# Middle passes of a two-layer decoder kernel: another order of calls on TensorE, ScalarE and VectorE, with key blocks around the turning of z0

## What is computed

```python
# layer 0
q, k, v = x @ kernel[0], x @ kernel[1], x @ kernel[2]      # 16 heads of 64
x = norm(x + softmax(q k / (d d h)) v @ WO)                # attention
x = norm(x + cross_attention(x, ctx))                      # 16 heads of 16, 120 context rows
x = norm(x + bitlinear(silu(bitlinear(x)) * bitlinear(x))) # rows quantized to 8 bit, weights to -1, 0, 1
# layer 1
h = norm(x); a = decay(h) @ (h @ Wv); x = x + sigmoid(h @ Wo) * a   # gated, causal
x = norm(x + mlp(norm(x)))
q = x @ Wq + bq; k1, k2 = ctx @ Wk1, ctx @ Wk2; v1, v2 = k1 @ Wv1, k2 @ Wv2
z0 = norm(q + softmax([q k1, q k2] / 16, axis=queries) [v1, v2]) * g0 + beta0
z1 = norm(z0 + relu(z0 @ Wo + bo)) * g1 + beta1;  x = norm(x + z1)
# coupled network: three cycles over the features, gf from the mean over the tokens
gf = sigmoid(g3(gelu(g2(gelu(g1(mean(x)))))))
for _ in range(3):
    tf = sigmoid(w4(gelu(w3(gelu(w2(gelu(w1(out))))))))
    out = out + (0.1 + range * (0.7 gf + 0.3 tf - 0.5) * 2) * twist(out)
x = norm(x + out)
```

## Time and profile before

| | us |
|---|---|
| median of 3 runs | 1095.97 (1095.93 to 1096.03) |
| the profiled execution, its own time | 1095.17 |
| its span, first to last instruction | 1093.4 |
| TensorE busy | 1023.6 (94% of the span) |
| VectorE busy | 793.0 (73%) |
| ScalarE busy | 629.3 (58%) |
| GpSimd busy | 310.2 (28%) |

### The profile page before, as it was taken

How to read it: one execution, slowest core, us unless ns; L and a number is a source line. 1 busy time by engine, 2 the same in 40 slices (tenths; PEclk the granted TensorE clock), 3 DMA queues, 4 the chain that set the end, 5 groups by cost and what they waited for, 6 DMA issues and landing times.

```text
span 1093.4 us, 19696 instructions
## 1 busy us (share of the span) xinstructions
PE 1023.6 (94%) x7216; PEld 686.6 (63%) x7224; DVE 793.0 (73%) x1854; ACT 629.3 (58%) x1720; POOL 310.2 (28%) x666
## 2 busy tenths in 40 slices
PE   9999999999989999999889999999988998799896
PEld 5577557855667655775557755786566675577563
DVE  3684886668697488657789578665869849865877
ACT  2583655476587257359468455646747816634933
POOL 1264202341056301242107420223104640124210
PEclk9999999999999999999999999999999999999998
DMA  9350000000010000000000000000000000000000
GB/s 338 83 170 1 20 1 10 1 1 1 1 40 1 20 2 10 1 1 1 1 20 21 1 20 1 10 1 1 1 0 11 12 1 1 1 1 0 2 1 20
DMA packets 16431, 22.78 MB, mean 21 GB/s; under 512 B 2256, under 2 KB 14032, under 8 KB 16208
## 3 DMA queue, kind: packets, MB, share of 16 engines
q1 hardware_dynamic: 15472, 20.85, 5.9%
q10 hardware_dynamic: 864, 0.68, 0.2%
HBM read 19.42 MB, written 2.10 MB: 20 GB/s over the span
## 4 chain that ended last, share of the span: by engine, by line
PE 62%; DVE 17%; ACT 12%; issue 5%; POOL 2%; DMA 1%; ACTq 0%; POOLq 0%; DVEq 0%
PE PS L542 9%; PE PS L970 4%; ACT work L1533 4%; PE PS L730 4%; PE PS L939 3%; PE PS L679 3%; PE PS L578 3%; PE PS L716 3%; ACT work L1787 3%; PE PS L565 2%; DVE maxx L2148 2%; PE PS L696 2%; PE PS L984 2%; DVE work L2165 2%; PE PS L1023 2%
## 5 line engine op out<-in xcount | busy, mean ns | idle before, releaser
L2628 POOL TENSOR_TENSOR rstd<-var,minus_half 128x2 f32<-128x2 f32 x64 | 45.8, 715 | 509.6 <-DVE var L1955 509.6
L1787 ACT ACTIVATE work<-PS,nmax 120x256 f32<-120x256 f32 x256 | 117.9, 484 | 13.6 <-DVE nmax L2443 12.6
L2443 DVE TENSOR_REDUCE nmax<-PS 120x2 f32<-120x512 f32 x128 | 82.5, 686 | 33.6 <-PE PS L970 32.5
L1533 ACT ACTIVATE work<-PS,nmax 128x256 f32<-128x256 f32 x176 | 81.6, 489 | 16.2 <-DVE nmax L2016 16.2
L2016 DVE TENSOR_REDUCE nmax<-PS 128x2 f32<-128x512 f32 x128 | 82.4, 679 | 10.9 <-PE PS L679 10.1
L2642 POOL TENSOR_SCALAR work<-work,inv 128x256 f32<-128x256 f32 x176 | 81.1, 479 | 0.0
L2623 POOL TENSOR_TENSOR pool_pause<-minus_half 128x1 f32<-128x1 f32 x96 | 28.5, 297 | 178.2 <-DVE inv L2023 92.4
L679 PE MATMUL PS<-work 64*128 64x256 f32 x512 | 72.2, 396 | 6.1 <-ACT work L1533 5.8
L1488 ACT COPY turned_a<-PS 128x512 f32<-128x512 f32 x24 | 14.2, 591 | 99.4 <-PE PS L519 99.3
L679 PEld LDWEIGHTS PS<-work 64*128 64x128 f32 x512 | 46.6, 186 | 22.8 <-ACT work L1533 15.1
L730 PE MATMUL PS<-wo,work 128*128 128x256 f32 x256 | 58.5, 384 | 0.0
(11 more groups left out here) (282 smaller groups left out, 2541.4 us busy)
## 6 DMA issues: line engine op xcount, KB each, us to landing
xa<-in_x_dram SPq DMA_DIRECT2D x4, 512.0 KB, 4.0
out_dram<-x_room SPq DMA_DIRECT2D x7, 256.0 KB, 2.2
rows<-in_rows_dram SPq DMA_DIRECT2D x1, 1536.0 KB, 10.9
turned_x<-in_x_turned_dram SPq DMA_DIRECT2D x3, 512.0 KB, 3.5
late<-in_L_attn_W_dram SPq DMA_DIRECT2D x2, 768.0 KB, 8.3
wq<-in_attn_q_dram SPq DMA_DIRECT2D x1, 1024.0 KB, 9.4
wk<-in_attn_k_dram SPq DMA_DIRECT2D x1, 1024.0 KB, 11.4
late<-in_ffn_gate_dram SPq DMA_DIRECT2D x1, 1024.0 KB, 13.5
```

Source lines behind the costliest of these rows:

```text
L1533: op = act.activation(e0[u % 3][:, st, hh, :], bank(2 * (u % 2) + hh)[:, st * S:(st + 1) * S], ACT.Exp, bias=nmax0[:, u % 2, hh, st:st + 1 ...
L1787: op = act.activation(e1[:, par, r, kv, :], bank(SCORE_1[r])[0:M, kv * S:(kv + 1) * S], ACT.Exp, bias=nmax1[:, par, r, kv:kv + 1], accum_o ...
L2443: dve.tensor_reduce(nmax1[:, par, r, :], bank(SCORE_1[r])[0:M, :].rearrange("p (v s) -> p v s", v=2), AX.X, ALU.max, negate=True).then_inc ...
```

## The change

Only orders of calls change; no instruction is added or taken away, and no size changes. It touches the functions for passes 0 to 2 (with `then`), the head of `attn0` in passes 1 to 3, and the place of one copy in ScalarE's `attn0` in all passes. Key block 4, so far wholly in `coupled_ffn`, has three of its quarters around the turning of z0 at the end of `cross1`, and the fourth behind `turn_c0(it, 0)`. In `coupled_ffn` the first steps of the coupled network follow each other without key quarters between them. The diff, cut to its changed lines with a line of context, the common indent taken off (the hunks are, in order: PE `coupled_ffn` twice, `attn0`, `cross0` twice, `ffn0` twice, `attn1`, `cross1` twice; ACT `attn0`, `cross0_ffn0` twice, `cross1` twice, `coupled_ffn`; DVE `cross1` twice, `coupled_ffn` twice):

```diff
@@ -1058,27 +1058,24 @@
     turn_c0(it, 0)
-    keys0(then, 4, (0,))
+    keys0(then, 4, (3,))
     net_1(it, 0)
-    global_net_1(it, 0, then)
     net_1_crossed(it, 0)
     net_2(it, 0, 0)
-    keys0(then, 4, (1,))
+    global_net_1(it, 0, then)
     global_net_2(it, 0)
+    net_3(it, 0, 0)
     turn_c0(it, 1)
-    keys0(then, 4, (2,))
-    net_3(it, 0, 0)
     global_net_3(it, 0)
...
     global_net_1(it, 1, then)
+    net_1_crossed(it, 1)
     net_2(it, 0, 1)
-    net_1_crossed(it, 1)
+    net_2(it, 1, 0)
     global_net_2(it, 1)
...
     global_net_3(it, 1)
-    keys0(then, 4, (3,))
-    net_2(it, 1, 0)
     net_4(it, 0, 1)
...
@@ -1086,8 +1083,8 @@
     keys0(then, 6, (0,))
+    keys0(then, 6, (1,))
     net_3(it, 1, 1)
-    keys0(then, 6, (1,))
     net_2(it, 2, 0)
...
@@ -1171,9 +1168,9 @@
         scores0(it, 2)
+        context0_keys(it, last)
         scores0(it, 3)
         turn0(it, 0, last)
-        context0_keys(it, last)
         scores0(it, 4)
...
@@ -1209,10 +1206,10 @@
     turn_normed(it, "x1", xs["1"], 1)
-    values0(then, 1, (0,))
     scores_x(it, 0)
...
     queries_x(it, 1)
+    values0(then, 1, (0,))
     scores_x(it, 2)
...
@@ -1221,8 +1218,8 @@
     weigh_x(it, 0, then)
+    turn_x(it, 3)
     scores_x(it, 5)
-    turn_x(it, 3)
     scores_x(it, 6)
...
@@ -1283,11 +1280,11 @@
     gate(it, 1)
+    values0(then, 7)
     up(it, 1)
-    values0(then, 7)
     gate(it, 2)
+    queries0(then, 0, (0,))
     up(it, 2)
-    queries0(then, 0, (0,))
     turn_hidden(it, 0)
...
@@ -1301,7 +1298,6 @@
     down(it, 2)
-    queries0(then, 3, (0,))
     down(it, 3)
...
@@ -1353,13 +1349,14 @@
     turn_normed(it, "h", xs["h"], 0)
+    queries0(then, 3, (0,))
     queries0(then, 3, (1,))
...
     turn_normed(it, "h", xs["h"], 1)
+    outputs_m(it, 0)
     queries0(then, 4)
     gates(it, 1)
-    outputs_m(it, 0)
     values_m(it, 1)
...
@@ -1380,12 +1377,11 @@
     queries0(then, 6, (1,))
+    turn_normed(it, "x4", xs["4"], 1)
     for n in range(0, GX * HC, 2):
         scores_1(it, n)
-        if n == 0:
-            turn_normed(it, "x4", xs["4"], 1)
-        if n in (0, 4):
-            queries0(then, 7, (n // 4,))
+        if n == 2:
+            queries0(then, 7)
         if n == 4:
...
@@ -1396,21 +1392,23 @@
             keys0_whole(then, 1, 0)
-        if n == 24:
+        if n % HP == 2 and HP < n < 24:
+            weigh_1(it, n // HP - 1)
+        if n == 26:
             turn_normed(it, "z0", aff, 0)
-        if n in (28, 30):
-            out_1(it, 0, ((n - 28) // 2,))
-        if n == 30:
-            keys0_whole(then, 1, 1)
-        if n % HP == 2 and n > HP:
-            weigh_1(it, n // HP - 1)
+        if n == 28:
+            weigh_1(it, 5)
+    out_1(it, 0)
+    keys0_whole(then, 1, 1)
+    weigh_1(it, 6)
     weigh_1(it, 2 * GX - 1)
+    keys0_whole(then, 2, 0)
     turn_back(it, 1)
-    keys0_whole(then, 2, 0)
     keys0_whole(then, 2, 1)
-    keys0(then, 3, (0, 1, 2))
+    keys0(then, 3)
+    keys0(then, 4, (0,))
     turn_normed(it, "z0", aff, 1)
-    keys0(then, 3, (3,))
+    keys0(then, 4, (1, 2))
     out_1(it, 1)
...
@@ -1562,19 +1560,20 @@
     else:
-        exp0(it, 0, (0,))
+        exp0(it, 0)
         keep_k0(it, J - 1)
-        exp0(it, 0, (1,))
         exp0(it, 1)
-        exp0(it, 2, (0,))
+        exp0(it, 2)
         keep_e0t(it, 0)
-        exp0(it, 2, (1,))
         exp0(it, 3)
...
         exp0(it, u, (0,))
-        keep_e0t(it, u - 2)
+        if u % 4:
+            keep_e0t(it, u - 2)
         exp0(it, u, (1,))
+        if u % 4 == 0:
+            keep_e0t(it, u - 2)
         exp0(it, u + 1)
...
@@ -1658,8 +1657,8 @@
         keep(it, "x1", 0)
+        keep_v0(then, 0)
         keep_queries(it, 0, 4, qx, col["L0_xattn_bq"], qx_done, qx_kept)
-        keep_v0(then, 0)
         keep(it, "x1", 1)
...
@@ -1690,8 +1689,8 @@
         keep_quantized(1)
+        keep_v0(then, 7)
         hidden_of(0)
-        keep_v0(then, 7)
         silu_of(2)
...
@@ -1774,7 +1773,7 @@
             keep(it, "x4", 1)
-        if n == (11 if then is not None else 14):
+        if n == (12 if then is not None else 14):
             keep_queries(it, 1, QUERY_1[1], q1, col["L1_xattn_bq"], q1_done, q1_kept)
...
@@ -1787,11 +1786,11 @@
         op.then_inc(p1_done.sem, 1)
-        if then is not None and n == 3:
+        if then is not None and n == 5:
             keep_q0(then, 7)
...
             keep_k0(then, 0)
-        if n == 25:
+        if n == 27:
             keep(it, "z0", 0)
...
@@ -1872,20 +1871,20 @@
         gelu_1(0, 0)
+        gelu_2(0, 0)
         global_1(0)
-        gelu_2(0, 0)
         global_2(0)
+        gelu_3(0, 0)
         keep_c0(1)
-        gelu_3(0, 0)
         global_3(0)
...
         global_1(1)
+        gelu_1(1, 0)
         gelu_2(0, 1)
+        keep_k0(then, 4)
         global_2(1)
-        gelu_1(1, 0)
         gelu_3(0, 1)
-        keep_k0(then, 4)
         global_3(1)
...
@@ -2454,14 +2453,17 @@
             continue
-        if n % HP == 1 and m:
-            scale_values(m - 1)
-        if n % HP == 3 and par == 0 and m > 1:
-            keep_o1(m // 2 - 1)
-        if n == GX // 2 * HC + 5:
+        if n == 29:
+            keep_o1(GX - 2)
+        if n in (5, 9, 13, 17, 21, 27, 29):
+            scale_values((n - 4) // HP)
+        if n in (11, 19):
+            keep_o1((n - 11) // HC)
+        if n == 21:
             stats_z0(0)
+        if n == 23:
             centre_z0(0)
-        if n == GX // 2 * HC + 7:
+        if n == 25:
             scale_z0(0)
...
@@ -2471,12 +2473,18 @@
     norm_summed(it, "z1", 0)
-    keep_o1(GX - 1)
-    centre_z1(0)
+    if it == NI - 1:
+        keep_o1(GX - 1)
+        centre_z1(0)
+    else:
+        centre_z1(0)
+        keep_o1(GX - 1)
+        sum_5(0)
     stats_z0(1)
...
     scale_z0(1)
-    sum_5(0)
+    if it == NI - 1:
+        sum_5(0)
     norm_summed(it, "5", 0)
...
@@ -2546,11 +2554,8 @@
     next_plain(it, 0, 1)
-    if then is None:
-        coupling(it, 1, 0)
+    coupling(it, 1, 0)
     next_crossed(it, 1)
-    if then is not None:
-        coupling(it, 1, 0)
     next_plain(it, 1, 0)
...
@@ -2562,12 +2567,9 @@
     sum_out(it, 0)
-    if then is not None:
-        norm_summed(it, "out", 0)
     coupling(it, 2, 1)
     next_state(it, 2, 1)
-    if then is None:
-        norm_summed(it, "out", 0)
+    norm_summed(it, "out", 0)
...
```

## The result

The changed kernel takes 1085.99 us (median; 1085.15 to 1089.07), the kernel before 1096.00 beside it: a ratio of 0.9914, interval 0.9894 to 0.9933. Its executions also differ by 3.9 us, those of the kernel before by 0.15.

The account below looks back on a forecast made before the run. TensorE, busy 94% of the span, was taken as the bound. Terms of -0.55, -0.2, +0.3, -0.4, -1.35 and +0.3 sum to -1.9 us a pass, -5.7 over three: 1095.97 becomes 1090.3 us, range 1087.0 to 1096.0.

Parts of the forecast that it names:

- cross1: Stage from first scores to turn_c0(0): earlier exponentials gain only 0.05, sum_5(0) leaves the chain; -0.4 us a pass.
- the loop of attn0: ScalarE's later copy at u = 4, 8, 12 costs nothing while two weigh0 cover it; 0 a pass.
- the coupled network: Stretch from turn_c0(0) to net_4(1, 0), 20.8 us, shortens without key quarters between steps; -1.35 us a pass.
- the head of attn0: Start of attn0: turn_final(1) starts 0.83 earlier, given back in later pauses; net +0.3 us a pass.
- ffn0 and attn1: ffn0: up(2) finds its product ready, -0.2 us a pass; attn1: down(3) pauses 0.5 uncovered, +0.3.
- cross0: Scores start 0.65 us earlier, the pause before turn_x(0) is filled; -0.55 us a pass, bounds -0.9 and 0.
- my walk: Queues followed in the new order with traced durations; for turn_c0(0) to the end of net_4(1, 0), 19.35 us.
- The caution: Coupled network: -1.35 us a pass was taken, between the walk and a quarter of caution.
- Rival (b): Coupled stretch keeps its length because turn_c0(1) comes from VectorE at the same time: 1094.4 us; chance 0.15.
- Rival (c): ScalarE's late copy at u = 4, 8, 12 of attn0 delays turn0, up to 10.8 us: 1101.1; chance 0.08.
- Rival (a): TensorE's clock falls behind net_4(1, 0), 1.7 us lost: 1092.0 in one pass, 1095.4 in three; chance 0.22.

Follow-up runs that it names:

- The start: Kernel before with only x4's second-batch turning ahead of cross1's scores, queries0(then, 7) whole after the second score pair, two ScalarE copies later: 1094.12 us against 1095.76.
- the middle: Kernel before with only cross1's z0 turning behind the 27th score, out_1(0) whole behind the scores, and VectorE's maxima reordered: 1093.89 us against 1095.20.
- the tail: Kernel before with only VectorE's order behind cross1's scores changed: keep_o1(GX - 1) behind centre_z1(0), sum_5(0) ahead of second-batch z0: 1096.12 us against 1095.76.

## Why the prediction was wrong in size

The forecast missed 2.6 us a pass: 0.8 in cross1, 0.7 in the loop of attn0, 0.6 in the coupled network, 0.3 in the head of attn0, and 0.25 in ffn0 and attn1. In cross1 and in the loop a step of the working was wrong; in the others a term was mis-sized.

- **cross0** was right to the last digit, in part by luck: -0.55. `turn_x(0)` has no pause, and the 0.36 at `turn_x(4)` is gone too, which was the bound of -0.9. But `turn_x(7)`, whose pause of 0.23 was to stay, waits for 0.68 and gives most of the difference back.
- **ffn0 and attn1:** the mechanism was right, `down(3)` waits; it waits 0.27 us and not 0.5, because the copy that it needs starts earlier too. +0.1 should have been -0.15.
- **cross1,** the step "`sum_z1(0)` waits for `out_1(0)` until about 522.2 as it did, so `scale_values(7)` and `weigh_1(7)` gain only 0.05". `out_1(0)` doesn't stand still: it is queued behind the scores, and the scores behind ScalarE. From the first scores to `sum_z1(0)` it was 784.59 - 748.41 = 36.2 us and is 778.15 - 743.06 = 35.1; 0.44 of the difference is the moved turning, 0.65 is gain. Nor was it `out_1(0)` that `sum_z1(0)` waited for in the kernel before: VectorE came to it from the last maximum without a pause, and the last maxima had waited for the scores. Only in the changed kernel does it wait for `out_1(0)` (L542), and earlier. I gave the earlier end of ScalarE's exponentials no effect and kept a TensorE call fixed that is queued behind them. The start (-0.46) and the middle (-0.32 to -0.5) are what that step set at 0.05. The stage's -1.18 lies beyond the bound of -1.0. For the tail I had 0.38; it is 0.28, and alone it is given back, because the chain to `turn_c0(1)` doesn't end earlier. The rows of `sum_z1(0)`, first the kernel before, then the changed one:

```profile
783.39 1.29 DVE L2443 TENSOR_REDUCE nmax<-PS 120x2 f32<-120x512 f32 x2 [0.39 <-PE PS L970]
784.59 0.68 DVE L2409 TENSOR_TENSOR res<-PS,rows 128x512 f32<-128x512 f32 x1
```

```profile
778.15 0.69 DVE L2408 TENSOR_TENSOR res<-PS,rows 128x512 f32<-128x512 f32 x1 [0.64 <-PE PS L542]
```

- **Coupled network:** my walk gave 19.35 us for the stretch, the nearest row, the last pass, 19.0, and it is 19.0. The walk counted pauses of 0.5 and 0.7 at `net_4(0, 1)` and `net_4(1, 0)`; they are 0.21 and 0.56. The caution taken off the walk's 1.45 had no row behind it: -1.35 should have been -1.94, the stage from `turn_c0(0)` to `turn_final(0)`. Rival (b) is out.
- **Head of attn0:** the mechanism was right, the lead is given back. Forecast were pauses of 0.5 at `scores0(2)`, 0.95 at `scores0(4)`, 0.35 at `turn0(1)` and 0.3 at `scores0(5)`; found 0.71, 0.65, none and 0.47. The term was 0.3 too high.
- **attn0's loop,** the step "costs nothing as long as the two `weigh0`, 1.95 us, cover half a unit and the copy". I asked only what the later copy would cost, and not what stood behind the earlier one. The row was there: the copy at 581.37 with 0.32 idle before it. A wait in an engine's queue ahead of work that is ready is the price of the old order; I used the row only for its 0.58. Rival (c) is out; the sign was the other way.
- **Rival (a)** came true in part. In the two profiles of the changed kernel the clock fell at the same place in five of the six middle passes, and I had 0.22 for it. The price was right and the place was not: I took the place from the last pass, whose `turn_c0(1)` doesn't wait so. The falls hid about a quarter of what the order won (3.3 of 13.8 us in the profile, the three passes' 13.6 and 0.16 of the last one's cross1); at full clock the forecast would have been off by some 8 us.
- **The range** ended at 1087.0, the sum of two terms at their better ends. Each term's better bound was named (-0.9, -0.2, -0.1, -1.0, -1.9, -0.8), three times their sum of -4.9 is 14.7 us, and I let all but two of them stay at their middles; the loop had no bound below nothing, though no reason excluded a gain.

## To carry over

When an instruction is moved back in an in-order queue, look first at whether it waits there: what stands behind it gains that wait and the instruction's own length, and a row with idle time ahead of a copy is where to begin. When independent work is taken out of a chain of short dependent steps, keep a quarter block of it for a place where two pauses come close together. Here, ahead of `turn_c0(1)`, it was free in the pause, and the clock stayed up in all six middle passes profiled with it. A stage's gain must be followed to the engine whose chain ends it, or it comes back as a longer wait one stage on, as in cross1's tail.
